# Two transformer layers on one core: loading, head projections and causal attention put into one block

## The reference

```python
qkv = jnp.einsum('bsi,oi->bso', x, w_qkv) + b_qkv
q, k, v = ...            # (batch 2, heads 16, 1024, 8) each
q = _rope(q, cos, sin)
k = _rope(k, cos, sin)
scores = jnp.einsum('bhqd,bhkd->bhqk', q, k) * scale
scores = jnp.where(causal, scores, jnp.finfo(jnp.float32).min)
ex = jnp.exp(scores - jnp.max(scores, axis=-1, keepdims=True))
attn = ex / (jnp.sum(ex, axis=-1, keepdims=True) + 1e-08)
o = jnp.einsum('bhqk,bhkd->bhqd', attn, v)
out = jnp.einsum('bsi,oi->bso', o, w_out) + b_out
```

## Time and profile before

| | us |
|---|---|
| median of 3 runs | 2374.53 (2363.93 to 2379.98) |
| the profiled execution | 2377.96 |
| its span | 2376.1 |
| PE busy | 2042.4 (86%) |
| DVE busy | 1836.0 (77%) |
| ACT busy | 1664.9 (70%) |
| POOL busy | 1230.2 (52%) |

### The profile page before, as it was taken

How to read it: one execution, slowest core, us unless ns; L and a number is a source line. 1 busy time by engine, 2 the same in 40 slices (tenths; PEclk the granted TensorE clock), 3 DMA queues, 4 the chain that set the end, 5 groups by cost and what they waited for, 6 DMA issues and landing times. The chain is left out here.

```text
span 2376.1 us, 55666 instructions
## 1 busy us (share of the span) xinstructions
PE 2042.4 (86%) x20349; PEld 1363.4 (57%) x20349; DVE 1836.0 (77%) x3651; ACT 1664.9 (70%) x3159; POOL 1230.2 (52%) x1102
## 2 busy tenths in 40 slices
PE   5279899858999999999999999999999999985274
PEld 2133333224677667776777667776777667763153
DVE  4555656069999999999999999999999999943623
ACT  2035555547888888888888888888888888863123
POOL 0200000057776777677776777677766777621042
PEclk9568989779999999999999999999999999996587
DMA  2522210021110102011110102011110101000511
GB/s 85 93 72 32 32 23 2 2 65 34 37 37 29 37 28 84 28 37 37 59 54 28 37 29 83 29 37 37 58 54 28 37 29 37 28 28 25 181 33 66
DMA packets 71492, 106.33 MB, mean 45 GB/s; under 512 B 21303, under 2 KB 45118, under 8 KB 70686
## 3 DMA queue, kind: packets, MB, share of 16 engines
q1 hardware_dynamic: 69942, 100.15, 15.4%
q0 software_dynamic: 1280, 2.62, 0.4%
HBM read 41.60 MB, written 11.21 MB: 22 GB/s over the span
## 5 line engine op out<-in xcount | busy, mean ns | idle before, releaser
L1393 POOL TENSOR_TENSOR qk<-rot_cos,rot_sin 128x512 f32<-128x512 f32 x256 | 323.7, 1276 | 160.3 <-DVE rot_sin L1194 160.3
L403 ACT ACTIVATE probs_by_key<-pT 128x512 f32<-128x512 f32 (+3 forms) x384 | 177.3, 490 | 228.5 <-PE pT L356 194.9
L1192 DVE TENSOR_TENSOR rot_cos<-pA,layer_tab 128x512 f32<-128x512 f32 x384 | 262.9, 685 | 66.5 <-ACT sq L1033 61.3
L1403 POOL TENSOR_TENSOR qk<-qk,rnorm 128x512 f32<-128x512 f32 x256 | 263.4, 1045 | 88.0 <-DVE rnorm L1227 88.0
L421 DVE TENSOR_REDUCE minus_max<-pS 128x1 f32<-128x1024 f32 (+7 forms) x256 | 184.6, 754 | 132.4 <-PE pS L330 132.2
L1033 ACT ACTIVATE sq<-pA 128x512 f32<-128x512 f32 x384 | 228.6, 596 | 56.3 <-PE pA L820 46.8
L1204 DVE TENSOR_REDUCE sumsq<-sq 128x8 f32<-128x512 f32 x384 | 253.4, 670 | 14.2 <-ACT sq L1033 14.1
L1194 DVE TENSOR_TENSOR rot_sin<-pA,layer_tab 128x512 f32<-128x512 f32 x384 | 260.8, 679 | 0.0
L1093 ACT ACTIVATE probsT<-pD 64x512 f32<-64x512 f32 x384 | 226.7, 590 | 44.0 <-PE pD L861 40.5
L1410 POOL TENSOR_TENSOR probs<-probs,row_inverse 128x1024 f32<-128x1024 f32 x96 | 182.9, 1906 | 102.4 <-DVE row_inverse L1263 102.4
L1053 ACT ACTIVATE qT<-pC 64x512 f32<-64x512 f32 x384 | 226.1, 589 | 7.4 <-PE pC L835 0.6
(11 more groups left out here) (292 smaller groups left out, 4679.9 us busy)
## 6 DMA issues: line engine op xcount, KB each, us to landing
v_shifted<-v SPq DMA_DIRECT2D x96, 384.0 KB, 3.5
v_shifted<-v SPq DMA_DIRECT2D x95, 128.0 KB, 3.4
q_stack<-stacked SPq DMA_DIRECT2D x72, 64.0 KB
k_stack<-stacked SPq DMA_DIRECT2D x72, 64.0 KB
W_ahead<-in_Wqkv_dram SPq DMA_DIRECT2D x12, 384.0 KB
layer_weights<-in_Wqkv_dram SPq DMA_DIRECT2D x12, 384.0 KB
stacked<-part SPq DMA_DIRECT2D x24, 128.0 KB, 1.9
tokens_in<-tokens SPq DMA_DIRECT2D x2, 1024.0 KB
```

The source lines that it names most:

```text
L1192: dve.tensor_tensor(t1[c % 2][:, :].rearrange("p (h g d) -> p h g d", g=2, d=32), a, tabl[s % 2][:, j].unsqueeze(1).broadcast_to([P, 8, 2, ...
L1393: pool.tensor_tensor(qk(s, c), t1[c % 2][:, :], t2[c % 2][:, :], ALU.add).then_inc(added[c], 1)
L1403: pool.tensor_tensor(v, v, rn[p % 2][:, o:o + 8].unsqueeze(2).broadcast_to([P, 8, DH]), ALU.mult).then_inc(scaled[c], 1)
```

## The change

`load_tokens`, `project_heads` and `causal_attention` become one function with one block, `causal_from_tokens`; `layernorm_all`, which nothing called, is removed.

- Loads: tokens and rotation table in halves with semaphores of their own; the seven loads of weights are issued by ACT; the output bias goes later into a freed row of `wr`.
- The first batch (c = 0, 1) is projected into all of PSUM. DVE adds the bias and multiplies with the table in one operation from PSUM, adds, and subtracts twice; ACT makes the bf16 casts.
- `stacked` has another layout in DRAM, with parts ahead of heads and, for the keys, parts 0 and 1 a second time, so that a group's nine loads a side become three of 24 partitions. All ones are set by GpSimd.
- The second batch's turning, all values and the second batch's projections are 14 jobs of PE and ACT: six ahead of the first score block, one behind each of the blocks 0, 2, ..., 14 of group 0. The first chunk waits for all jobs.
- GpSimd rotates and splits the second batch (7 operations for each of four pairs). SP stores them behind the maxima of group 0 and of group 1. The value bias is added where GpSimd copies values.
- The block's semaphores stay allocated until the window layers' end and are cleared there.

```diff
-def project_heads(nc, env, w, V):
...
-def causal_attention(nc, env, w, V, O):
+def causal_from_tokens(nc, env, w, V, O):
...
+        raw = [sb(f"raw{r}", [P, 4, 512]) for r in range(2)]
+        rot = sb("rot", [P, 2, 512])
+        left = sb("left", [P, 2, 512])
+        parts = [[[sb(f"part{r}{m}{j}", [P, 512], BF16) for j in range(PARTS)] for m in range(2)] for r in range(2)]
...
-        NLD = 2 * PARTS * PARTS
+        NLD = 2 * PARTS
+        JOBS = [("turn", 2), ("turn", 3), ("v", 0), ("v", 1)] + [("qk", c, m) for c in (2, 3) for m in range(4)] + [("v", 2), ("v", 3)]
+        NJ, EARLY_JOBS = len(JOBS), 6
+        BANKS = ST + OT
+        FIRST = [BANKS, [S[m // 2][:, 512 * (m % 2):512 * (m % 2) + 512] for m in range(4)]]
+        STORED = 16 * 2 * (PARTS + 2 * PARTS - 1)
...
-                r0, c0, r = (g % 4) * (GH * AD), (g // 4) * SEQ, g % SLOTS_G
-                sp.wait_ge(ones_set[r % 2], r // 2 + 1)
+                r, n = g % SLOTS_G, PARTS * AD
+                q, key = (w["stacked"][m, g // 4, :, :, (g % 4) * GH:(g % 4 + 1) * GH, :].rearrange("k d h n -> (k d) h n") for m in range(2))
+                sp.wait_ge(ones_set, r + 1)
+                sp.wait_ge(stored[g // 4], STORED)
                 ge(sp, st_ready, NT * (g - SLOTS_G + 1))
-                for j in range(PARTS):
-                    for k in range(PARTS):
-                        at = (j * PARTS + k) * AD
-                        sp.dma_start(QS[r][at:at + AD, :, :], w["stacked"][0, j, r0:r0 + GH * AD, c0:c0 + SEQ].rearrange("(h d) n -> d h n", d=AD))\
-                            .then_inc(stacks[r], 16)
-                        sp.dma_start(KS[r][at:at + AD, :, :], w["stacked"][1, k, r0:r0 + GH * AD, c0:c0 + SEQ].rearrange("(h d) n -> d h n", d=AD))\
-                            .then_inc(stacks[r], 16)
+                for b in range(PARTS):
+                    sp.dma_start(QS[r][b * n:(b + 1) * n, :, :], q[0:n]).then_inc(stacks[r], 16)
+                    sp.dma_start(KS[r][b * n:(b + 1) * n, :, :], key[b * AD:b * AD + n]).then_inc(stacks[r], 16)
...
+            def store(c, m, j):
+                for i in (j, j + PARTS) if m and j < PARTS - 1 else (j,):
+                    sp.dma_start(w["stacked"][m, c // 2, i, :, :, 512 * (c % 2):512 * (c % 2) + 512].rearrange("d h n -> h d n"),
+                                 parts[c % 2][m][j][:, :]).then_inc(stored[c // 2], 16)
+            def load_rope(r):
+                sp.dma_start(rope[:, :, 512 * r:512 * r + 512], w["rope"][:, :, 512 * r:512 * r + 512]).then_inc(rope_in[r], 16)
+            def load_tokens(r):
+                sp.dma_start(X[:, TB * r:TB * r + TB, :], w["x"][SEQ * r:SEQ * r + SEQ, :].rearrange("(t p) d -> p t d", p=P)).then_inc(x_in[r], 16)
+            def late_stores(c):
+                for m in range(2):
+                    sp.wait_ge(late_split, 2 * (c - 2) + m + 1)
+                    for j in range(PARTS):
+                        store(c, m, j)
+            bqkv = w["a_b_qkv"]
+            sp.dma_start(ident[:, :], w["identity"]).then_inc(x_in[0], 16)
+            load_tokens(0)
+            load_rope(0)
+            ...
+            load_rope(1)
+            load_tokens(1)
             sp.dma_start(cm[:, :, :], w["causal"]).then_inc(mask_in, 16)
+            sp.dma_start(bv[:, :], bqkv[2 * D:3 * D].rearrange("(a n) -> a n", a=1).broadcast_to([P, D])).then_inc(bv_in, 16)
+            sp.dma_start(env["wo"][:, :], w["a_w_out"]).then_inc(env["out_loaded"], 16)
+            for c in range(2):
+                for j in range(PARTS - 1):
+                    for m in range(2):
+                        sp.wait_ge(cast, 4 * c + 2 * j + m + 1)
+                        store(c, m, j)
+                for m in range(2):
+                    sp.wait_ge(split, 2 * c + m + 1)
+                    store(c, m, PARTS - 1)
             for g in range(SLOTS_G):
                 load_stacks(g)
+            sp.wait_ge(w_turned, 2)
+            sp.dma_start(wr[:, 0, :], w["a_b_out"].rearrange("(a n) -> a n", a=1).broadcast_to([P, D])).then_inc(bo_in, 16)
...
                 load_maxima(g)
+                if g < 2:
+                    late_stores(2 + g)
...
+            def job(j):
+                kind, out = JOBS[j], BANKS[j % 4]
+                if j < 4:
+                    pe.wait_ge(rotated, j // 2 + 1)
+                else:
+                    pe.wait_ge(job_kept, j - 3)
+                if kind[0] == "turn":
+                    pe.wait_ge(x_in[1], 16)
+                    mm = turn_tokens(kind[1], out)
+                elif kind[0] == "qk":
+                    mm = project(kind[1], kind[2], out)
+                else:
+                    for i in range(4):
+                        t = 4 * kind[1] + i
+                        mm = pe.matmul(out[:, i * P:(i + 1) * P], xT[:, t * P:(t + 1) * P], wT[:, 4, :], start=True, stop=True,
+                                       skip_group_check=True)
+                mm.then_inc(job_ready, 1)
+            pe.wait_ge(x_in[0], 32)
+            for n in range(2):
+                turn_tokens(n, S[0][:, 512 * n:512 * n + 512]).then_inc(x_turned, 1)
...
+            for c in range(2):
+                for m in range(4):
+                    project(c, m, FIRST[c][m]).then_inc(qk_ready, 1)
...
+            for j in range(EARLY_JOBS):
+                job(j)
+                    if it == 0 and u % 2 == 0 and EARLY_JOBS + u // 2 < NJ:
+                        job(EARLY_JOBS + u // 2)
...
+            for m, row in enumerate((0, 0, D, D, 2 * D)):
+                ...
+                    act.dma_start(wr[:, m, :], src).then_inc(w_in, 16)
+            ...
+            for c in range(2):
+                for m in range(2):
+                    act.wait_ge(rotated, 2 * c + m + 1)
+                    act.activation(parts[c][m][0][:, :], rot[:, m, :], AF.Copy).then_inc(cast, 1)
+                for m in range(2):
+                    act.wait_ge(rest, 2 * c + m + 1)
+                    act.activation(parts[c][m][1][:, :], left[:, m, :], AF.Copy).then_inc(cast, 1)
+            for j, kind in enumerate(JOBS):
+                act.wait_ge(job_ready, j + 1)
+                if kind[0] == "turn":
+                    act.activation(xT[:, 512 * kind[1]:512 * kind[1] + 512], BANKS[j % 4][:, :], AF.Copy).then_inc(job_kept, 1)
+                elif kind[0] == "qk":
+                    act.wait_ge(bias_in, 16 * 6)
+                    act.activation(raw[kind[1] - 2][:, kind[2], :], BANKS[j % 4][:, :], AF.Identity, bias=bias[:, kind[2]:kind[2] + 1])\
+                        .then_inc(job_kept, 1)
...
+            def scale(c, m):
+                if c:
+                    dve.wait_ge(split, m + 1)
+                for k in range(2):
+                    dve.wait_ge(qk_ready, 4 * c + 2 * m + k + 1)
+                    dve.scalar_tensor_tensor((rot, left)[k][:, m, :], FIRST[c][2 * m + k][:, :], bias[:, 2 * m + k:2 * m + k + 1],
+                                             rope[:, k, 512 * c:512 * c + 512], ALU.add, ALU.mult).then_inc(scaled, 1)
+            def rotate(c, m):
+                dve.wait_ge(scaled, 4 * c + 2 * m + 2)
+                dve.tensor_tensor(rot[:, m, :], rot[:, m, :], left[:, m, :], ALU.add).then_inc(rotated, 1)
+            def first_rest(c, m):
+                dve.wait_ge(cast, 4 * c + m + 1)
+                dve.tensor_tensor(left[:, m, :], rot[:, m, :], parts[c][m][0][:, :], ALU.subtract).then_inc(rest, 1)
+            def last_part(c, m):
+                dve.wait_ge(cast, 4 * c + m + 3)
+                dve.tensor_tensor(parts[c][m][2][:, :], left[:, m, :], parts[c][m][1][:, :], ALU.subtract).then_inc(split, 1)
...
+            scale(0, 0)
+            scale(0, 1)
+            rotate(0, 0)
+            rotate(0, 1)
+            first_rest(0, 0)
+            first_rest(0, 1)
+            last_part(0, 0)
+            dve.wait_ge(rope_in[1], 16)
+            scale(1, 0)
+            last_part(0, 1)
+            scale(1, 1)
+            rotate(1, 0)
+            rotate(1, 1)
+            first_rest(1, 0)
+            first_rest(1, 1)
+            last_part(1, 0)
+            last_part(1, 1)
...
+            def copy_values(g):
+                r0, c0 = (g // 4) * TB, (g % 4) * (GH * AD)
+                pool.tensor_tensor(Vs[g % 2][:, :, :, 0:AD], V[:, r0:r0 + TB, c0:c0 + GH * AD].rearrange("p t (h d) -> p t h d", h=GH),
+                                   bv[:, c0:c0 + GH * AD].rearrange("p (h d) -> p h d", h=GH).unsqueeze(1).broadcast_to([P, TB, GH, AD]), ALU.add)\
+                    .then_inc(v_copied, 1)
+            pool.wait_ge(bv_in, 16)
+            pool.wait_ge(job_kept, 4)
+            copy_values(0)
+            copy_values(1)
+            pool.wait_ge(stored[0], STORED)
+            for r in range(2):
+                pool.wait_ge(rope_in[r], 16)
+            n = 0
+            for c in range(2):
+                pool.wait_ge(job_kept, 8 + 4 * c)
+                for m in range(2):
```

(75 more changed lines are left out.)

189 lines of the change are left out of this document (45 added, 144 removed).

## The result

| | before | after |
|---|---|---|
| median, us | 2377.26 (2363.93 to 2387.8, 4 runs) | 2307.02 (2305.42 to 2315.78, 4 runs) |
| span of the profiled execution | 2376.1 | 2305.3 |

What follows compares the result with a forecast made beforehand. Before 91 us the path was loads, DVE, block end and stack loads, then the scores, with PE the limit from 150. Terms -49+6-3 = -46 on the median 2374.53 gave 2328.5, called 2330, range 2306 to 2354.

Steps and rivals of the forecast that it cites:

- parts 1 to 3: Opening: earlier loads, fewer DVE operations for one batch, stores, then stack loads; first score at 42 instead of 91.1, minus 49.
- Stack loads: Before the first score: six loads of 192 KB replace eighteen of 64 KB, 10 us from issue to score instead of 18.2.
- engine rule of the Trainium skill: Stack loads: engines used divide the slowest dimension, 12 for 24 rows; 12.8 us, making the gain 3 us smaller.
- Jobs, plus 6: Group 0: eight jobs of PE and ACT between the first score blocks add 6 us at the low clock.
- rival B: First scores: clock high from about 45 on, jobs free and big blocks shorter, 2313 us; chance 0.13.
- Maxima, minus 3: Near 143: PE's 3.4 us wait for maxima queued behind layer weights goes, as those loads come some 20 us earlier.
- GpSimd, nothing: Second batch's rotation and split on GpSimd, 28 operations of 1.28 us from about 46 to 82, cost nothing.
- rival C: Attention: more low-clock stretches, or stack loads at 18 us and all jobs exposed, give 2345 to 2358; chance 0.18.
- D (GpSimd late): Second batch's split: GpSimd far slower, holding up SP's queue; 1% lost only near 6.8 us an operation (2400); chance 0.04.
- E (opening hidden): Opening: it is hidden anyway, so the time stays at 2374; chance 0.03.

Runs made afterwards that it cites:

- experiment 2: The changed kernel with each group's stacks filled by eighteen loads of 8 partitions again instead of six of 24: 2343.61 us, ratio 0.9866.
- experiment 3: The kernel before with only the new DRAM layout, eight more key stores and six stack loads of 24 partitions a group: 2357.97 us, ratio 0.9927.
- experiment 4: The kernel before with the first window layer's weights and two constant tables issued behind group 0's maxima: 2370.15 us against 2377.70, ratio 0.9970.
- experiment 5: The changed kernel with all fourteen jobs ahead of the first score block: 2307.52 us, ratio 0.9703.
- experiment 6: The changed kernel without GpSimd's 28 operations that rotate and split the second batch (wrong results): 2306.46 us, ratio 0.9698.
- experiment 7: Six extra matmuls a group at group ends: kernel before 2371.71 us (0.9988), changed kernel 2303.68 (0.9691), changed kernel with all jobs first 2308.83 (0.9701).

## Why the prediction was right, and where its sizes were off

- **Loads, DVE's share, stores** (parts 1 to 3): right to within 1 us. DVE could start at 12.99 (forecast 12.3), the split ended at 28.4 (29), the first stack load went out at 32.60 (32). The fused operation takes 0.75, not 0.69.
- **Stack loads**: 9.4 us (10), held up from both sides by experiments 2 and 3. That the size was so close is in part luck: the 9.6 us worked out for it from 123 GB/s leave out the 1.9 us to landing that the two other estimates have, so they should have been 11.5, and the rate was 162, not 123. The gain was a little larger than 49, as the first score at 91.1 was an early one: 93.8, 93.9 and 94.8 in three later traces with the old loads, 93.4 in the mean, against 42.2 in the mean of five with the new ones. The engine rule of the Trainium skill that the prediction cites (DMA: Bandwidth & Descriptors) fits the shares, 0.51 of sixteen engines with 8 partitions and 0.73 with 24, but the 12.8 us estimated by it don't hold: the rate rose 2.45 times with 1.5 times the engines, so each engine was faster too.
- **Jobs, plus 6**: the term that was mis-sized with the wrong sign. Group 0 became 2.7 us shorter (31.5, where about 40 was forecast). The forecast had the low clock of the earlier trace rows go on while the jobs made PE busy; rival B had the high one, for the whole group. What came lies between: 1.00 in the window at 50, 0.50 from 64.
- **Maxima, minus 3**: the mechanism was right, the size came from one execution. The wait was 3.4, 10.4 and 13.7 us in the three traces with the old opening and order, and group 1 took 41.5, 51.2 and 51.3 against 40.5 and 40.6 after. Without the wait (experiment 4) it took 37.9, so the wait is worth 10 us in the mean; group 1 gained 7 of them, as GpSimd took the rest.
- **GpSimd, nothing**: the 28 operations took 1.26 or 1.16 us (1.28 forecast), the casts, for which the forecast had no row, 0.61, and they ended at 78.4 (82):

```profile
L522 POOL TENSOR_TENSOR rot<-raw,rope_tab 128x512 f32<-128x512 f32 x4 | 5.0, 1262 | 16.7 <-ACT raw L367 16.7
...
L527 POOL CAST part<-rot 128x512 bf16<-128x512 f32 x4 | 2.4, 609 | 0.3
```

  But "DVE's reductions beside it read PSUM" left out DVE's four small operations at the group's end, for which PE waits: plus 2.2 to 2.7 us (experiments 5 and 6).
- **Falls of the clock**: rival C let them take from the gain and read the row at 220 as a fall of a fully busy PE. The fall had begun behind a group's end, and in the two traces compared the falls added 20 us to the gain. Over all traces without extra matmuls, six groups took 238.5 to 250.5 us in the four with the old opening (243.4 on average) and 230.4 to 237.3 in the five with the new one (233.2). So some 10 us of the gain are fewer falls, as far as nine traces tell; taking the falls away from the kernel before (experiment 7) should then have brought 13 us and brought 2.5 in the median, its interval reaching to 12.

In these means 51 for the first score, 2.7 for group 0, 7 for group 1 and 10 for the later groups, less 1 in the last chunks, are 70, and 65 to 70 were measured. That the time lies inside the range is partly luck as well. Its lower end was set by rival B and loads of 6 us, neither of which came; the time got there by the sign of the jobs, the maxima and the falls, which the sum had at plus 6, minus 3 and nothing. The rivals D (GpSimd late) and E (opening hidden) are ruled out by GpSimd's end and by the first score.

**What stays open:** why the kernels with the old opening have more falls (12 of 24 groups against 5 of 30), and whether that holds over many executions. The extra matmuls show that the falls hang on PE's idling at group ends, but that idling is the same in both kernels. The one trace of experiment 2 speaks against the number of loads. What shifts the odds between the two kernels was not tried.

## What to carry to other kernels

Forecast an opening by its path: which load ends last, the vector engine's chain, the last store, the first load back. That was good to a microsecond here where each term had its row. A wait behind an engine that is still issuing bulk loads is a sample and not a size; ask what it would be if those issues ran a few microseconds later, and move bulk loads for later stages behind the small transfer that somebody needs now. And when work is moved onto GpSimd, look for the vector engine's small SBUF operations in that stretch, not at its long ones alone.

## What the runs showed of the hardware that was not expected

- A DVE cast of 128x32 that takes 0.18 us alone took 1.08 beside GpSimd's addition. The cast of the identity (128x128) took 0.23 at 7.83 in the kernel before and 2.44 at 5.43 beside GpSimd's memset in the kernel after. Both ended with GpSimd's operation.
- Loads of 64 KB into 8 partitions each ran at 66 GB/s, loads of 192 KB into 24 at 162, from the same rows of 8 KB.
- SP needed 16.9 us behind the stack loads for four issues of 384 KB that took 1.8 with no bulk load ahead of them (experiments 2 and 4).
- Behind group ends at which PE was busy 2.86 of 4 us, the granted clock fell in 17 of 54 cases, and in none of 24 with one more matmul of 512 columns ahead of each of six chunks.
